# Attention of a sandwich layer: numbering by group, three key/query slots, and a first group whose steps carry more of the later groups' maxima

## What is computed

```python
c_kv = x @ W_dkv.T
q = (x @ W_dq.T @ W_uq.T).reshape(B, T, nh, hs).transpose(0, 2, 1, 3)
q_lat = jnp.einsum('bhtd,hdl->bhtl', q, k_eff)
attn = jnp.einsum('bhtl,bsl->bhts', q_lat, c_kv) / math.sqrt(hs)
attn = jnp.where(causal_mask[None, None], -jnp.inf, attn)
attn = jax.nn.softmax(attn, axis=-1)
ctx = jnp.einsum('bhts,bsl->bhtl', attn, c_kv)
```

## Time and profile before

| | us |
|---|---|
| median of three runs (lowest, highest) | 1288.51 (1287.94, 1291.63) |
| the profiled execution, its own time | 1288.09 |
| its span in the trace | 1286.4 |
| ahead of the first step: attention block from its start | 100.4 to 136.9 |
| one group of steps, groups 0 to 13 | 31.4 |
| all of attention | 100 to 638 |

### The profile page before, as it was taken

One profiled execution on the slowest core, in us unless ns is written; L12 is line 12 of the kernel. 1 busy time (PEld: TensorE's weight loads), 2 busy tenths in 40 slices (PEclk: granted clock), 3 DMA queues, 4 the chain that ended last, 5 costly groups with the idle time before them and its releaser, 6 DMA issues. The chain is left out here.

```text
span 1286.4 us, 24447 instructions
## 1 busy us (share of the span) xinstructions
PE 1055.7 (82%) x7329; PEld 807.5 (63%) x7329; DVE 824.0 (64%) x2492; ACT 640.9 (50%) x1111; POOL 587.7 (46%) x675
## 2 busy tenths in 40 slices
PE   5979999999999999998633512999999999999900
PEld 2535555555555555554223512999999999999900
DVE  5738877777777777773188521556555655565577
ACT  2640566666666666667544421445444444444533
POOL 4205466665556555556647772223223222232237
PEclk9985899999999999999855555999999999999955
DMA  4986244444454444422272235242542414321173
GB/s 137 373 298 195 94 159 158 159 158 159 162 171 169 168 167 170 167 100 103 98 251 77 74 136 180 70 145 81 185 166 59 176 49 176 137 88 49 42 269 131
DMA packets 93849, 190.03 MB, mean 148 GB/s; under 512 B 27480, under 2 KB 58600, under 8 KB 85512
## 3 DMA queue, kind: packets, MB, share of 16 engines
q1 hardware_dynamic: 82920, 163.22, 36.5%
q0 software_dynamic: 7680, 22.09, 4.9%
q10 hardware_dynamic: 3176, 3.84, 1.1%
HBM read 109.54 MB, written 79.05 MB: 147 GB/s over the span
## 5 line engine op out<-in xcount | busy, mean ns | idle before, releaser
L777 ACT ACTIVATE att_pt<-att_ps_s 128x1024 f32<-128x1024 f32 (+3 forms) x384 | 297.8, 815 | 179.8 <-PE att_ps_s L692 176.3
L804 DVE CUSTOM_DVE_ANT_0 att_ps_m<-att_ps_m,keep_future 128x384 f32<-128x384 f32 (+2 forms) x384 | 204.2, 585 | 77.4 <-PE att_ps_m L655 77.4
L1520 ACT ACTIVATE moe_hf<-moe_ps_h,moe_b 128x256 f32<-128x256 f32 x288 | 134.3, 475 | 225.2 <-PE moe_ps_h L1476 211.2
L655 PE MATMUL att_ps_m<-att_k,att_q 128*128 128x512 f32 (+3 forms) x576 | 180.0, 386 | 5.5 <-DVE att_pm L804 4.3
L813 DVE TENSOR_REDUCE att_pm<-att_ps_m 128x1 f32<-128x512 f32 x256 | 161.4, 684 | 21.4 <-PE att_ps_m L655 21.4
L600 POOL TENSOR_SCALAR_AFFINE_SELECT att_pt<-att_pt 128x512 f32<-128x512 f32 x128 | 81.7, 639 | 185.2 <-ACT att_pt L777 185.2
L692 PE MATMUL att_ps_s<-att_q,att_k 128*128 128x512 f32 (+3 forms) x576 | 155.9, 360 | 6.2 <-ACT att_pt L777 5.1
L1429 POOL DMA_INDIRECT ys<-moe_o,moe_home x72 | 73.9, 1026 | 184.4 <-DVE moe_o L1559 171.5
L692 PEld LDWEIGHTS att_ps_s<-att_q,att_k 128*128 128x128 f32 x576 | 95.2, 188 | 56.4 <-issue 28.9
L1553 DVE TENSOR_TENSOR moe_hTl<-moe_hf,moe_hTh 128x256 fp32r<-128x256 f32 x288 | 124.0, 431 | 10.0 <-DVE moe_hTh L1551 0.2
L655 PEld LDWEIGHTS att_ps_m<-att_k,att_q 128*128 128x128 f32 x576 | 99.1, 194 | 47.9 <-DVE att_pm L804 15.4
(11 more groups left out here) (197 smaller groups left out, 2507.2 us busy)
## 6 DMA issues: line engine op xcount, KB each, us to landing
att_raw<-in_w SPq DMA_DIRECT2D x16, 1024.0 KB, 5.1
ws<-att_raw_hi SPq DMA_DIRECT2D x16, 1024.0 KB, 3.9
ws<-att_raw SPq DMA_DIRECT2D x16, 1024.0 KB, 5.9
moe_rows<-xs SPq DMA_DIRECT2D x38, 258.0 KB
att_q<-qs SPq DMA_DIRECT2D x33, 256.0 KB
att_k<-ks SPq DMA_DIRECT2D x66, 128.0 KB
weights_w_0h<-ws SPq DMA_DIRECT2D x8, 1024.0 KB
weights_w_0l<-ws SPq DMA_DIRECT2D x8, 1024.0 KB
```

The source lines that it names most:

```text
L655: ins = pe.matmul(out[:, end - keys:end], qg[slot][:, h // 2, i * P:(i + 1) * P], kg[slot][:, h, k0:k0 + keys], start=not whole, stop=not ...
L777: act.activation(pt[:, blk % NPT, 2 * p:2 * p + 2, off:CH], ps_s[k % 2][:, :, off:CH], ACT.Exp, scale=HS ** -0.5).then_inc(ex_done, 1)
L804: ins = dve.tensor_tensor_reduce(part, part, future[:, CH - keys:CH], 1.0, LOWEST, ALU.add, ALU.max, pm[:, g % 2, 0, head, place:place + 1])
L1520: act.activation(hf[:, f % NHB], ps_h[f % NHB][:], ACT.Relu, bias=b1[r][:, f:f + 1]).then_inc(hf_done, 1)
```

## The change

The kernel numbers everything by group, 0 to 15, and SP's loop over the sequences is written out. What changes in the order and in the buffers:

- `first` becomes `FIRST`: the 38 units of group 0 and one turn. The 18 units of group 1 that stood there go into the steps: the steps of group 0 carry 49 units (`DEALT_FIRST`: all 38 of group 1 and 11 of group 2), those of group 1 carry 45 (`DEALT_SECOND`: 27 of group 2 and 18 of group 3). From group 2 on `DEALT` and its 18 units ahead are as before.
- In group 0 the turn of group 1 stands at step 20; in all others it stays at step 17.
- The second, empty entry of the turn is gone, on PE and on ACT.
- NSL = 3 slots. In the steps of group g SP loads group g+2 into the slot of g-1; the place in SP's order and the condition (the values of g-1 done) are as before. Slot 3, its two memsets and its rows of ones are gone. At the start SP writes the rows of group 0 first, waits until group 1 is loaded, then loads group 2 and fetches the first raw weights.
- DMA addresses of SP are constants instead of registers.

```diff
-NSL = NG
+NSL = 3
-LOADS = 16 * (3 + 2 * 3 + 2) // NSL
+LOADS = 16 * (3 + 2 * 3 + 2)
-HALF = NU // 4 * 2
+AHEAD = 18
+DEALT_FIRST = ((0, 0), (1, 0), (2, 0), (2, 0), (2, 0), (1, 2), (2, 0), (2, 0), (2, 0), (1, 2), (2, 0), (2, 0),
+               (2, 0), (1, 2), (2, 0), (2, 0), (2, 0), (1, 2), (2, 0), (2, 0), (1, 0), (1, 2), (2, 0), (2, 0))
+DEALT_SECOND = ((2, 0), (1, 2), (2, 0), (2, 0), (2, 0), (1, 1), (2, 0), (1, 0), (2, 0), (1, 2), (2, 0), (2, 0),
+                (2, 0), (1, 1), (1, 0), (2, 0), (2, 0), (1, 1), (2, 0), (2, 0), (2, 0), (1, 1), (1, 0), (0, 0))
...
+def all_jobs():
+    first = [(("unit", 0, m), m) for m in range(NU)] + [(("turn", 0, 0), NU)]
+    number = len(first)
+    units = [("unit", g, m) for g in range(1, GROUPS) for m in range(NU)]
+    groups = []
+    for g in range(GROUPS):
+        steps = []
+        for k, (early, late) in enumerate((DEALT_FIRST, DEALT_SECOND)[g] if g < 2 else DEALT):
+            step = Step()
+            steps.append(step)
+            for jobs, count in ((step.early, early), (step.late, late)):
+                for _ in range(count):
+                    if units and units[0][1] <= g + 2 and not (units[0][1] == g + 2 and units[0][2] >= AHEAD):
+                        jobs.append((units.pop(0), number))
+                        number += 1
+                if jobs is step.early:
+                    more = [("out", g, c) for c in range(2) if k == OUT_STEPS[c] and g + c > 0]
+                    more += [("turn", g + 1, 0)] if k == (20 if g == 0 else 17) and g + 1 < GROUPS else []
...
                 for u in range(2):
                     sp.wait_ge(keep["stored"][u], STORES * B + 1)
-                max_rows(0, 0, first.index(("turn", 0, 0)))
-                sp.wait_ge(slots["init"][3], 2)
-                load_ones(sp, d, slots, 3)
-                fetch_raw(0, 0)
+                max_rows(0)
+                sp.wait_ge(*group_in(1))
+                load_group(sp, d, slots, 2)
+                fetch_raw(0)
+                for g in range(GROUPS):
+                    if 0 < g < GROUPS - 2:
+                        sp.wait_ge(pv_done, g * NB)
+                        load_group(sp, d, slots, g + 2)
+                    if g + 1 < GROUPS:
+                        max_rows(g + 1)
+                    keep_split(g)
...
-                def max_turn(b, g, half, out):
-                    if half == 1:
-                        return pe.nop()
```

More of the change, by code:

```diff
@@ L2 @@
 from contextlib import ExitStack
-from itertools import islice
 import numpy as np
@@ L388 @@
 DIAG = [n for n, (c, j) in enumerate(BLOCKS) if j >= c * TC]
+PASSES = {4 * n + 1: (2 * n - 2, 2 * n - 1) for n in range(NB // 2)}
 def max_units():
@@ L425, in unit_keys, with __init__, all @@
     return len(heads) * sum(keys for _, _, keys, _ in pieces)
[L428 to L450, removed]
+class Step:
+    def __init__(self):
+        self.early, self.late = [], []
+    def all(self):
+        return self.early + self.late
+def all_jobs():
[16 more added lines that the diff above has]
+                    more += [("turn", g + 1, 0)] if k == (20 if g == 0 else 17) and g + 1 < GROUPS else []
+                    for job in more:
+                        jobs.append((job, number))
+                        number += 1
+        groups.append(steps)
+    assert not units
+    return first, groups, (("out", GROUPS, 0), number)
+GROUPS = B * NG
+FIRST, DEAL, LAST = all_jobs()
+NUMBER = {job: n for job, n in [*FIRST, *(j for steps in DEAL for step in steps for j in step.all())]}
 def attend(nc, d, keep, slots):
@@ L486, in attend, with made, read, group_in @@
         pm_done, nh_hi, nh_done = (s.sem(n) for n in ("pm_done", "nh_hi", "nh_done"))
[L489 to L516, removed]
+        def made(n):
+            return bank_made[n % NBK], n // NBK + 1
+        def read(n):
+            return bank_read[n % NBK], n // NBK + 1
+        def group_in(g):
+            return loaded[g % NSL], ONES + (g // NSL + 1) * LOADS
+        def rows_in(g):
+            return m_in[g % NSL], (g // NSL + 1) * 64
         with nc.Block() as block:
@@ L610, in split, with unit @@
                         part = slice(n * HALF_W // 2, (n + 1) * HALF_W // 2)
-                        pool.wait_ge(split_hi, at(b, g, 2, n + 1))
+                        pool.wait_ge(split_hi, 2 * g + n + 1)
                         pool.tensor_tensor(raw[:, part].bitcast(F32R), raw[:, part], raw_hi[:, part], ALU.subtract
                                            ).then_inc(split_lo, 1)
[L615 to L626, removed]
+                for g, steps in enumerate(DEAL):
+                    for k, step in enumerate(steps):
+                        if k == TB:
+                            split(g)
+                        if k % 2 == 1 and k // 2 in DIAG:
+                            clear(g, k // 2)
+                        for what, n in step.all():
+                            if what[0] == "out":
+                                divide(g, what[2], n)
+                divide(GROUPS, 0, LAST[1])
             @block.tensor
             def _(pe):
[L630 to L640, removed]
+                def unit(g, m, out):
                     heads, pieces = UNITS[m]
@@ L734, in _ @@
+                pe.matmul(ps_o[:], onesb[:, 0:P], onesb[:], start=True, stop=True)
+                jobs(FIRST)
+                for g, steps in enumerate(DEAL):
+                    for k, step in enumerate(steps):
+                        scores(g, k)
+                        jobs(step.early)
+                        if k in PASSES:
+                            values_pass(g, k)
+                        jobs(step.late)
+                values_pass(GROUPS, 1)
+                jobs([LAST])
             @block.scalar
@@ L789, in _ @@
-                for b in range(B):
-                    body(b)
-                keep_out(B, 0, 0)
-                keep_sums(B - 1, NG, 0, numbered(B - 1)[1])
+                fill_mt(0, NUMBER["turn", 0, 0])
+                for g, steps in enumerate(DEAL):
+                    for k, (c, j, p) in enumerate(STEPS):
+                        blk = g * NB + k // 2
+                        act.wait_ge(st_made, g * NS + k + 1)
+                        if blk >= NPT:
+                            act.wait_ge(pv_done, blk - NPT + 1)
+                        off = max(0, (j - c * TC) * P)
+                        act.activation(pt[:, blk % NPT, 2 * p:2 * p + 2, off:CH], ps_s[k % 2][:, :, off:CH],
+                                       ACT.Exp, scale=HS ** -0.5).then_inc(ex_done, 1)
+                        if k == 2 and g > 0:
+                            keep_out(g, 0)
+                        if k == 10:
+                            keep_out(g, 1)
+                        for what, n in steps[k].all():
+                            if what[0] == "turn":
+                                fill_mt(what[1], n)
+                            if what[0] == "out":
+                                keep_sums(g, what[2], n)
```

245 lines of the change are left out of this document (99 added, 146 removed).

## The result

The change makes the kernel slower by 0.4%: the median of eight runs is 1295.05 us (1294.41 to 1298.47) against 1290.28 us (1287.94 to 1291.63) for the kernel before in eight runs. The ratio is 1.0041, with a 95% interval of 1.0032 to 1.0050. The forecast was 0.9991 of the median before (1287.3 us), with a range up to 1.0039 (1293.5 us), so the time lies above the range, on the other side of no change. The kernel before itself came out 1.8 us higher in these eight runs than in the three that the forecast started from, so of the 7.8 us between 1287.3 and 1295.05 some 6 are the change's; the ratio doesn't depend on this.

The account below looks back on a forecast made before the run. PE was taken to bound the steps, DVE the units ahead of them. Terms -5.2 + 5.6 + 1.0 - 5.2 + 1.0 + 1.0 + 0.6 gave -1.2 us: median 1287.3 us, range 1282.5 to 1293.5.

Parts of the forecast that it names:

- first scores earlier: Start of the steps: first scores at 131.7 instead of 136.9 us, a gain of 5.2 us.
- 18 units, DVE, clock and turn in groups 0 and 1: Steps of groups 0 and 1: units +5.6, slower DVE +1.0, low clock +1.0, group 1's turn +1.0 us.
- empty entry gone: Turn at step 17: PE no longer waits for a bank, 0.39 us in up to 14 groups; taken as -5.2 us.
- three slots: Unit 0 of group g+2, step 11: can wait for its later load, about 1 us late in two groups; +0.6 us.
- The half turn: PE's turn at step 17: dropping its empty second entry saves 0.39 us a group, which nothing following on PE takes back.
- 18 x 0.31: Units moved into the steps of groups 0 and 1: each costs PE's 0.31 us, +5.6 us (bounds 4.1 and 11.5).
- loads become the bound: Rival at unit 0 of the group after next, step 11: all 12 groups wait, +9 us, about 1296; chance 0.12.
- DVE or the clock rules group 0: Rival in group 0: DVE bounds half the extra units, clock and turn cost more; 5.5 us over the sum, 1292.8; chance 0.1.
- Today PE is never idle: Ahead of the first step: PE has no idle time before the change, 4.4 us after; low clock then costs +1.0 us.

Follow-up runs that it names:

- e8: Changed kernel with four slots, 7 units of group 1 on PE while group 0's rows travel, the other 11 in the steps; ratio 0.9971 to the kernel before.
- e7: Changed kernel with four slots, DVE taking unmasked maxima over only 256 of 512 columns in groups 1 to 3; ratio 0.9981 to the kernel before.
- e1: Changed kernel with a fourth slot again, each load one group earlier; ratio 1.0005 to the kernel before.
- e5: Changed kernel with four slots and 9 unread matmuls on PE between group 0's turn and the first scores; ratio 0.9989 to the kernel before.
- e6: Changed kernel with four slots, DVE joining group 1's maxima right behind that group's last unit; ratio 1.0009 to the kernel before.
- e2: Changed kernel with 18 units of group 1 back ahead of the first step, every group dealt as before, three slots; ratio 0.9987 to the kernel before.

## Why the prediction was wrong

The balance of attention, each term as it was forecast and as the traces have it:

| term | forecast | measured |
|---|---|---|
| first scores earlier | -5.2 | -5.9 (136.88 to 130.95) |
| 18 units, DVE, clock and turn in groups 0 and 1 | +8.6 | +12.5 (39.25 and 35.3 against 31.05 each) |
| empty entry gone | -5.2 | -5.2 (14 x 0.37); put back alone in 12 groups: +3.4, with load waits 1.0 shorter |
| three slots | +0.6 | +3.5 (0.3, 1.8, 0.6, 0.8 us) |
| sum | -1.2 | +4.9; attention ended 4.96 us later |

**Right.** The start came as worked out: turn at 126.78 for 127.0, issue at 127.46 for 127.7, first scores 0.75 us before the forecast. The half turn held to a tenth (0.37 us a group): nothing behind it on PE took the saving back.

**Wrong: "18 x 0.31".** The step that failed is the price of a unit. I took PE's, "since PE is the fuller engine" (it read 97% busy), and set DVE's share apart as +1.0. In group 1, where the clock is at its full level and neither the gap nor the late turn lies, 7 extra units cost 35.3 - 31.05 = 4.2 us, 0.6 each. That is nearly DVE's 0.64 from the earlier trace rows, the end of the range that I had named and not taken. e8 gives 0.5 each, dealt otherwise. e7 divides the 4.2 us: a lighter DVE gives back 1.7 with PE's work unchanged, and the 2.5 that stay are 0.36 a unit. So PE's price was near what a unit costs where DVE has room; the other 0.24 goes when DVE's work falls from 29.5 to 24.9 us, and that share the forecast had too small. At 0.5 to 0.6, 18 units cost 9 to 11 us, where the forecast had 6.6 and the early start brings 5.9. Group 0 took 8.2 us more for 11 units, where the clock (an estimate of up to some 2 us, from e1) and DVE's lag at the turn come on top. Busy time of PE misled me: for 7 units more it grew from 30.5 to 34.2 us.

**Wrong in size: the loads.** The mechanism was named, and the place and the point from which it decides (21.1 us behind the rows) were right: undisturbed groups have unit 0 there (261.51 to 282.62). But the term was 0.6 us and measured 3.5. Two readings were short. First, no row had shown the 0.4 us from the last traffic to the release; in the four waiting groups it was 0.6 to 0.7 (the traffic ends at 377.0, unit 0 is at 377.61). Second, I took the load as ended where the dense traffic ends. In four of the twelve loads before the change a thin stream of some 15 to 30 GB/s runs on behind it for 0.7 to 1.2 us. The load that I put at about 244.6, 20.3 us behind its rows, so ends at 245.7, 21.3 behind. A window of the kernel before, its last column in GB/s:

```profile
244.90:245.60 0.70, 0.70 (x4) 0.37 (x2) 0.70 (x3) 0.70 (x1) 0.70 (x2) 1.00 0.08 18
```

Read to the end of that stream, six of the twelve loads lay at 21.2 us or later before the change, and not two. After the change the loads come earlier: SP issues a load's last DMA 15.6 us behind the rows where it took 17.0 (groups of the rows at 323.59 and 318.61). I put this down to the constant addresses; no run separates it. Three of the twelve then end at 20.9 to 21.4 us and one at 22.3, and these four are the waits. The rival ("loads become the bound", all 12 groups, +9) was too strong, the sum too weak.

**The range.** The two misses are +3.9 us (12.5 for 8.6) and +2.9 us. The second rival, "DVE or the clock rules group 0", had the first of them nearly right: it put those terms at 14.1 us, with a chance of 0.1. Each miss alone would have stayed well within the range. Together, less the 0.7 us of the better start, they come to 1287.3 + 6.1 = 1293.4, its upper edge: I had priced the rivals one at a time.

**The gap.** The Trainium skill, "TensorE: Matmul & The Clock Gate" (Why this matters for your kernels), advises against idle gaps of PE between bursts. Here the group behind the gap did spend 6.6 us at the lower level, against 1.0 before. But these runs don't show that the gap is the cause, so they neither bear the advice out nor refute it here. In the kernel before, where PE stood at most 0.7 us at a time in the 12 us ahead of the first step, the clock fell as well, at 131.1, and stayed down until 137.9. Windows of the kernel before on both sides of the fall:

```profile
127.70:131.00 3.30, 1.71 (x7) 0.85 (x7) 2.95 (x15) 0.27 (x1) 0.00 (x0) 1.00 0.01 2
131.10:137.90 6.80, 6.78 (x14) 3.42 (x13) 6.72 (x18) 0.00 (x0) 0.00 (x0) 0.50 0.50 154
```

The low stretch was there already; only its last 1.0 us lay behind the first step. In the changed kernel it runs from 127.3 to 137.5, and the steps begin inside it. With the gap filled it is there too: e5's clock did not rise for its products, and in e8 it fell at 126.7 and rose at 133.5, with PE busy 4.0 of 4.2 us of the gap. "Today PE is never idle" in the prediction is not exact either: PE was busy 10.69 of the 12.3 us ahead of the first step.

**Open.** How the remaining cost of group 0 divides between the clock and the dealing. e5 was to tell and could not, and e1, e5, e6 and the changed kernel differ in when the clock rises (134.9 to 137.6) without an edit that sets it. Each kernel has one trace, so how much of this differs from one execution to the next isn't known.

## What to carry to other kernels

Moving work from an idle stretch into a busy pipeline is priced at what one more piece costs there. Here that was 0.5 to 0.6 us a unit, and not the 0.31 of the matmul engine alone, though that one read 97% busy: the second engine that the unit loads, busy for 84% of the group, added to the price. An experiment that lightens one engine and leaves the other's work shows the shares; busy time doesn't. A slot fewer is free only if the load that it delays ends ahead of its use in every round, slowest included; read the slowest rounds, read each load to the last of its traffic, thin or dense, and add what lies between that and the release. An empty entry in a rotation of buffers isn't free either: it held PE 0.37 us in each group for a bank that nobody wanted.

## What the runs showed that I had not expected

- PE's busy share doesn't tell at which level the clock stands: PE read as busy 4.0 of 4.0 us at 0.50 in e5's gap, 24.0 of 24.2 us at 0.50 in the earlier trace rows, and 30.5 of 31.4 us at 1.00 in the steps there.
- The slow load returns in the same group. Its issue of rows is the one at 350.00 before, 354.65 after, 348.02 in e2: the interval behind it is 32.86 us after the change and 32.88 in e2, the longest of the later ones in both. There the two stores of split weights ahead of the load took until 365.16, 7.8 us from the second's issue at 357.34, where the next group's took 6.0 (390.21 to 396.18).
